# Sending for constants, attention weights and row vectors after the first tile's x has landed

## The chip, the cores and the metric
The kernel runs on one core of a Trainium2 chip. The metric is the device time of one execution in microseconds (us), smaller being better.

## The reference
For an input H of 16 batches x 512 tokens x 256 features (f32) the kernel computes

```
xn  = layernorm(x)                               # no gain, no bias
qkv = xn @ W_qkv.T + b_qkv ; q = elu(q)+1 ; k = elu(k)+1        # 16 heads of 16
att = (q @ (k.T @ v)) / clip(q . sum(k), 1e-6)                  # linear attention
a   = layernorm(att @ W_proj.T + b_proj) * gamma + beta + xn
h   = silu((xn @ w1.T) * s1) * ((xn @ w2.T) * s2)               # 256 -> 1024
h   = gelu((h @ h1.T) * t1) ; h = gelu((h @ h2.T) * t2)         # 1024 -> 1024, twice
out = x + a + (h @ w3.T) * s3                                   # 1024 -> 256
```

w1, w2, h1, h2 and w3 hold only -1, 0 and 1.

## The kernel before, in words
A tile is one batch of 512 tokens; 16 tiles go through a loop on every engine (`over_tiles`: a prologue for the first tile, then a body for each). Every engine has its program written out by hand, and the engines are tied by semaphores alone. The FFN weights (11.5 MB) stay in SBUF for the whole run. An activation that enters a matmul is split in two parts (high bits and remainder), so the attention projections are three matmuls per product (lines 391 to 393) and an FFN product is two (L386).

In the body the attention steps of the next tile stand between FFN groups, so TensorE always finds work. Only the first tile has a prologue in the open, and this is where the change lies:

- SyncE (SP) sends for the first tile's x (L296), then for the half of the row vectors that holds the k and v bias (L326, 256 KB, one row repeated on 128 partitions), the vectors of per-feature scales and the q bias (L327), the other row vectors (L328, 512 KB), and a first 176 KB piece of the raw weights (L306), which VectorE later checks for low bits.
- ScalarE (ACT) sends for the constants (L593: identity and head masks), the raw qkv weights (L594, 768 KB) and the raw projection weights (L595, 256 KB). It then waits for the qkv weights and casts them into their high part (L598). **Behind that it waits for the vectors (L599)**, and only then comes to `transposed_hi` (L627), the high part of the transposed xn.
- GpSimd (POOL) waits for x (L342), sends for the first 2 MB of the FFN weights (L346), computes the first tile's 1/sqrt(var) (L353) and sends for the other five pieces (L346 again).
- VectorE (DVE) waits for x, makes the layer norm (L708, L701, L703, L714), then the low part of the qkv weights (L850, after ScalarE's cast), then the low part of the transposed xn (L727).
- TensorE (PE) runs five warm-up matmuls (L377), waits for constants and xn, transposes xn (L401), waits for both parts of the qkv weights and of the transposed xn, and runs the projections of the first tile (L391 to L393); then the body begins.

The lines that a sentence can't replace are ScalarE's start:

```
593  act.dma_start(const[:], consts).then_inc(s_const, 16)
594  act.dma_start(wqkv_raw[:]..., w_attn[:, 0:DC * 3 * D]).then_inc(s_qkv_raw, 16)
595  act.dma_start(wproj_raw[:]..., w_attn[:, DC * 3 * D:]).then_inc(s_proj_raw, 16)
597  act.wait_ge(s_qkv_raw, 16)
598  nc.scalar.activation(wqkv[:, 0], wqkv_raw[:], ACT.Copy).then_inc(s_hi_w, 1)
599  act.wait_ge(s_vec, 16)
```

Of the kernel before, what the change touches and what calls it, by code (L numbers as in the profile page):

```python
# [98 lines left out]
def block_kernel(nc, H, w_ffn, w_attn, vecs, rows, consts, out):  # L99
# [70 lines left out]
    def sem(name):  # L170
        return nc.alloc_semaphore(name)
# [23 lines left out]
    x_loaded = Count(sem("x_loaded"), 1, unit=16)  # L195
# [77 lines left out]
    def over_tiles(eng, first, prologue, body):  # L273

        prologue(first)
        with eng.Fori(first, first + B - 1) as t:
            body(t, True)
        body(first + B - 1, False)

    def second_pass_if_needed(eng, run):  # L280
        eng.wait_ge(s_flag, 1)
        need = eng.value_load(flag[0:1, 0:1])
        with eng.If(need != 0):
            run()

    block = nc.Block()
    with block:


        @block.sync  # L290
        def _(sp):
            sp.sem_inc(acc_free.sem, 1)

            def load_x(t, first):
                sp.wait_ge(acc_made.sem, acc_made.at(t - 1, TC - 1))
                sp.dma_start(x[:], of_tile(x_dram, t - first)).then_inc(x_loaded.sem, 16)  # L296

            def of_tile(dram, tile):
                return dram[tile] if isinstance(tile, int) else dram[bass.ds(tile, 1)][0]

            def body_of(first):
                def load_piece(t, j):
                    sp.wait_ge(piece_checked.sem, piece_checked.at(t, j - 1))
                    col = (t * CHECKS + j) * CHECK_COLS
                    src = w_ffn[:, col:col + CHECK_COLS] if isinstance(col, int) else w_ffn[:, bass.ds(col, CHECK_COLS)]
                    sp.dma_start(raw[:], src.bitcast(U32)).then_inc(piece_loaded.sem, 16)  # L306

                def body(t, more):
                    if first == 0:
                        load_piece(t, 0)  # L310
                    if more:
                        load_x(t + 1, first)
                    if first == 0:
                        for j in range(1, CHECKS):
                            load_piece(t, j)
                    for half in range(2):
                        two = slice(2 * half, 2 * half + 2)
                        sp.wait_ge(out_made.sem, out_made.at(t, half))
                        sp.dma_start(of_tile(out_dram, t - first)[:, two], acc[:, two]).then_inc(out_stored.sem, 16)
                    sp.wait_ge(out_stored.sem, out_stored.at(t, 1))  # L320
                    sp.sem_inc(acc_free.sem, 1)
                return body

            def prologue(t):
                load_x(t, 0)
                sp.dma_start(rowv[:, R_BKV:], rows[:, R_BKV:].to_broadcast([P, 2 * D])).then_inc(s_bias_kv, 16)  # L326
                sp.dma_start(vec[:], vecs).then_inc(s_vec, 16)  # L327
                sp.dma_start(rowv[:, :R_BKV], rows[:, :R_BKV].to_broadcast([P, R_BKV])).then_inc(s_rows, 16)  # L328

            over_tiles(sp, 0, prologue, body_of(0))  # L330

            def second():
                sp.dma_start(w_full[:], w_ffn).then_inc(s_reload, 16)
                over_tiles(sp, B, lambda t: load_x(t, B), body_of(B))
            second_pass_if_needed(sp, second)
# [254 lines left out]

        @block.scalar
        def _(act):
            act.dma_start(const[:], consts).then_inc(s_const, 16)  # L593
            act.dma_start(wqkv_raw[:].rearrange("p k n -> p (k n)"), w_attn[:, 0:DC * 3 * D]).then_inc(s_qkv_raw, 16)  # L594
            act.dma_start(wproj_raw[:].rearrange("p k n -> p (k n)"), w_attn[:, DC * 3 * D:]).then_inc(s_proj_raw, 16)  # L595
# [402 lines left out]
```

## Time and profile before

| what | value |
|---|---|
| device time, median of 3 runs | 1606.58 us (1605.88 to 1607.11) |
| span of the profiled execution, first to last instruction | 1605.2 us |
| TensorE busy | 99% of the span |
| mean granted TensorE clock | 0.997 |
| x of the first tile, from issue to landing | 7.4 us |
| same transfer for the other tiles | 3.4 to 3.7 us |

The profiled execution has no device time of its own beside its span; the span is 1.4 us under the median of the timed runs. A span runs from the first instruction to the last. In the profile a DMA is issued by an engine's sequencer (SPq, ACTq, POOL) and is worked off by 16 DMA engines that all queues share: queue q1 is SP's, q10 is ACT's, q0 is POOL's. A "packet" of the DMA views is one piece of a transfer: here a stretch that is contiguous on one partition. x has four of 1 KB on each of 128 partitions; the other loads have one on each, so 128 packets, 8 on each of 16 engines.

### The profile page before, as it was taken

What the parts mean: (1) busy time and instruction counts of PE and PEld (TensorE: products, weight loads), DVE (VectorE), ACT (ScalarE), POOL (GpSimd) and SP (SyncE); (2) the same over time, 40 slices, a digit from 0 to 9 for tenths busy, and PEclk for the clock granted to TensorE, in tenths of its full rate; (3) what the DMA queues carried; (4) which work ended last, traced back from release to release, by engine and by line L of the source; (5) the groups of instructions that cost most, each with busy time, mean ns of one, the idle gap of its engine ahead of it and who ended that gap; (6) DMA issues with size and microseconds to landing.
All of it is one profiled execution on the core that took longest, in us unless ns stands there. A gap on an engine that the chain in (4) does not pass through costs nothing.

```text
span 1605.2 us, 22443 instructions
## 1 busy us (share of the span) xinstructions
PE 1591.0 (99%) x7884; PEld 1326.0 (83%) x7884; DVE 945.4 (59%) x1927; ACT 527.6 (33%) x817; POOL 38.1 (2%) x44
## 2 busy tenths in 40 slices
PE   8999999999999999999999999999999999999998
PEld 5888888888888888888888888888888888888886
DVE  5656657466564656647566474664746646566563
ACT  3324142241423424233242332423324143241421
POOL 1000000000000000000000000000000000000000
PEclk9999999999999999999999999999999999999999
DMA  9000000000000000000000000000000000000000
GB/s 355 23 12 11 27 18 22 11 11 27 18 22 18 4 27 18 22 22 0 27 18 27 18 9 18 18 27 18 18 9 18 27 18 22 11 11 27 18 10 20
DMA packets 28114, 42.07 MB, mean 26 GB/s; under 512 B 2112, under 2 KB 26816, under 8 KB 27328
## 3 DMA queue, kind: packets, MB, share of 16 engines
q1 hardware_dynamic: 26800, 29.12, 5.7%
q0 software_dynamic: 864, 11.53, 1.8%
q10 hardware_dynamic: 432, 1.18, 0.2%
q8 instruction: 10, 0.16, 0.0%
q14 instruction: 8, 0.07, 0.0%
HBM read 33.44 MB, written 8.39 MB: 26 GB/s over the span
## 4 chain that ended last, share of the span: by engine, by line
PE 99%; DMA 0%; DVE 0%; POOL 0%; issue 0%; DVEq 0%; POOLq 0%
PE ps L386 74%; PE ps L519 7%; PE ps L391 4%; PE ps L392 4%; PE ps L393 4%; PE ps L442 2%; PE ps L431 2%; PE ps L452 1%; PE ps L401 1%; DMA x<-in_H 0%; DVE wqkv_parts L850 0%; DVE xn L714 0%; DVE bn_stats L708 0%; POOL rstd L353 0%; DVE xn L837 0%
## 5 line engine op out<-in xcount | busy, mean ns | idle before, releaser
L386 PE MATMUL ps<-hidden_a,w_ffn 128*128 128x512 f32 x2048 | 488.1, 397 | 0.0
L386 PE MATMUL ps<-hidden_b,w_ffn 128*128 128x512 f32 x2048 | 484.4, 396 | 0.0
L386 PEld LDWEIGHTS ps<-hidden_b,w_ffn 128*128 128x128 f32 x2048 | 383.5, 188 | 91.6
L386 PEld LDWEIGHTS ps<-hidden_a,w_ffn 128*128 128x128 f32 x2048 | 381.4, 188 | 88.5
L622 ACT ACTIVATE value_ring<-ps,vectors 128x512 f32<-128x512 f32 x256 | 173.1, 689 | 693.7 <-PE ps L386 684.4
L386 PE MATMUL ps<-xnT,w_ffn 128*128 128x512 f32 x1024 | 249.4, 398 | 0.0
L386 PEld LDWEIGHTS ps<-xnT,w_ffn 128*128 128x128 f32 x1024 | 190.1, 188 | 43.6
L803 DVE CAST hidden_a<-value_ring 128x512 fp32r<-128x512 f32 x128 | 54.5, 426 | 216.0 <-ACT value_ring L622 216.0
L789 DVE SCALAR_TENSOR_TENSOR value_ring<-ps,vectors,gate_ring 128x512 f32<-128x512 f32 x128 | 94.2, 746 | 83.5 <-ACT gate_ring L604 83.5
L519 PEld LDWEIGHTS ps<-w_ffn,hidden_a 128*128 128x128 f32 x1024 | 123.9, 188 | 2.9
L519 PE MATMUL ps<-w_ffn,hidden_a 128*128 128x256 f32 x1024 | 124.6, 279 | 0.0
L803 DVE CAST hidden_b<-value_ring 128x512 fp32r<-128x512 f32 x128 | 54.5, 425 | 113.6 <-ACT value_ring L622 113.3
L604 ACT ACTIVATE gate_ring<-ps,vectors 128x512 f32<-128x512 f32 x128 | 86.7, 689 | 99.2 <-PE ps L386 99.0
L805 DVE TENSOR_TENSOR hidden_b<-value_ring,hidden_b 128x512 fp32r<-128x512 f32 x128 | 88.6, 692 | 4.4
L805 DVE TENSOR_TENSOR hidden_a<-value_ring,hidden_a 128x512 fp32r<-128x512 f32 x128 | 88.6, 692 | 4.4
L794 DVE TENSOR_TENSOR hidden_a<-value_ring,hidden_a 128x512 fp32r<-128x512 f32 x128 | 87.4, 683 | 2.2
L609 ACT ACTIVATE hidden_a<-value_ring 128x512 fp32r<-128x512 f32 x128 | 80.0, 625 | 9.7 <-DVE value_ring L789 9.7
L639 ACT ACTIVATE exp_tmp<-zkv 128x256 f32<-128x256 f32 x64 | 26.8, 418 | 150.1 <-DVE zkv L739 150.1
L845 DVE SCALAR_TENSOR_TENSOR low_bits<-raw_weights,low_bits 128x352 uint32<-128x352 uint32 x64 | 33.5, 523 | 68.7 <-DMA raw_weights<-in_w_ffn 68.7
L353 POOL TENSOR_TENSOR rstd<-var_plus_eps,power 128x4 f32<-128x4 f32 x32 | 34.3, 1072 | 1503.1 <-DVE var_plus_eps L703 1503.1
L739 DVE TENSOR_TENSOR zkv<-ps,row_vectors 128x512 f32<-128x512 f32 x64 | 44.3, 692 | 22.4 <-PE ps L393 22.4
L837 DVE TENSOR_TENSOR xn<-ps,row_vectors 128x512 f32<-128x512 f32 x32 | 22.1, 692 | 49.3 <-PE ps L519 49.3
(76 smaller groups left out, 1338.8 us busy)
## 6 DMA issues: line engine op xcount, KB each, us to landing
raw_weights<-in_w_ffn SPq DMA_DIRECT2D x64, 176.0 KB, 2.3
w_ffn<-in_w_ffn POOLq DMA_DIRECT2D x5, 2048.0 KB, 14.0
x<-in_H SPq DMA_DIRECT2D x16, 512.0 KB, 3.6
out_dram<-acc SPq DMA_DIRECT2D x32, 256.0 KB, 2.2
w_ffn<-in_w_ffn POOLq DMA_DIRECT2D x1, 1024.0 KB, 24.6
wqkv_raw<-in_w_attn ACTq DMA_DIRECT2D x1, 768.0 KB, 5.5
row_vectors<-in_rows SPq DMA_DIRECT2D x1, 512.0 KB, 7.8
wproj_raw<-in_w_attn ACTq DMA_DIRECT2D x1, 256.0 KB, 6.8
```

Of the source, the lines that this page charges most:

```text
L386: r = mm(bank, a, b, start=first and part == 0, stop=last and part == 1)
L391: mm(bank, wl, xh, start=first, stop=False)
L392: mm(bank, wh, xl, start=False, stop=False)
L393: return mm(bank, wh, xh, start=False, stop=last)
L519: r = mm(pair_bank(g, j)[:, 0:D], f(a) if full else a, wk, start=k == 0 and part == 0, stop=k == HC - 1 and part == 1)
L604: nc.scalar.activation(gate[:, o % 2, :], pair_bank(o, 0), ACT.Silu, scale=vec[:, V_GATE + o:V_GATE + o + 1]).then_inc(silu_made.sem, 1)
L609: nc.scalar.activation(ha[:, o, 0, :], val[:, o % 2, :], ACT.Copy).then_inc(gate_hi.sem, 1)
L622: nc.scalar.activation(val[:, n % 2, :], pair_bank(g, j), ACT.Gelu, scale=vec[:, col:col + 1]).then_inc(gelu_made.sem, 1)
L789: v.scalar_tensor_tensor(out=val[:, o % 2, :], in0=pair_bank(o, 1), scalar=vec[:, V_UP + o:V_UP + o + 1], in1=gate[:, o % 2, :], op0=ALU.m ...
L794: v.tensor_tensor(ha[:, o, 1, :], val[:, o % 2, :], ha[:, o, 0, :].bitcast(F32), ALU.subtract).then_inc(split.sem, 1)
L803: v.tensor_copy(dst[:, o, 0, :], val[:, n % 2, :]).then_inc(hid_hi.sem, 1)
L805: v.tensor_tensor(dst[:, o, 1, :], val[:, n % 2, :], dst[:, o, 0, :].bitcast(F32), ALU.subtract).then_inc(split.sem, 1)
```

## The change
SP waits for the first x to have landed before it issues its three other loads of the prologue, and ACT waits for the same before it issues its three. The order within each queue stays, and no load, size or arithmetic changes. POOL's wait for x stood there before.

```diff
             def prologue(t):
                 load_x(t, 0)
+                sp.wait_ge(x_loaded.sem, x_loaded.at(t, 0))
                 sp.dma_start(rowv[:, R_BKV:], rows[:, R_BKV:].to_broadcast([P, 2 * D])).then_inc(s_bias_kv, 16)
                 sp.dma_start(vec[:], vecs).then_inc(s_vec, 16)
                 sp.dma_start(rowv[:, :R_BKV], rows[:, :R_BKV].to_broadcast([P, R_BKV])).then_inc(s_rows, 16)
...
         def _(act):
+            act.wait_ge(x_loaded.sem, x_loaded.at(0, 0))
             act.dma_start(const[:], consts).then_inc(s_const, 16)
             act.dma_start(wqkv_raw[:].rearrange("p k n -> p (k n)"), w_attn[:, 0:DC * 3 * D]).then_inc(s_qkv_raw, 16)
             act.dma_start(wproj_raw[:].rearrange("p k n -> p (k n)"), w_attn[:, DC * 3 * D:]).then_inc(s_proj_raw, 16)
```

On ScalarE, at the very start of its program, before the change (with what each instruction waits for):

```order
L593 DMA constants<-in_consts 128x264
L594 DMA wqkv_raw<-in_w_attn 128x1536
L595 DMA wproj_raw<-in_w_attn 128x512
L598 ACT_TABLE_LOAD
L598 ACTIVATE wqkv_parts<-wqkv_raw 128x1536 [waits qkv_weights_loaded]
L627 ACTIVATE xnT<-ps 128x512 [waits attention_step_ready,vectors_loaded]
```

The same place now (line numbers are two higher behind the two new lines):

```order
L595 DMA constants<-in_consts 128x264 [waits x_loaded]
L596 DMA wqkv_raw<-in_w_attn 128x1536
L597 DMA wproj_raw<-in_w_attn 128x512
L600 ACT_TABLE_LOAD
L600 ACTIVATE wqkv_parts<-wqkv_raw 128x1536 [waits qkv_weights_loaded]
L629 ACTIVATE xnT<-ps 128x512 [waits attention_step_ready,vectors_loaded]
```

The first DMA of the three has gained the wait, and all that stands behind it on ScalarE is held with it.

On SyncE, the start of its program now; before, the second row had no wait and nothing else was different:

```order
L296 DMA x<-in_H 128x4x256 [waits acc_made]
L327 DMA row_vectors<-in_rows 128x512 [waits x_loaded]
L328 DMA vectors<-in_vecs 128x34
L329 DMA row_vectors<-in_rows 128x1024
```

The loads of the row vectors and vectors, and the raw weights' first piece behind them, have moved behind x's landing. GpSimd's start, with the same wait in both kernels (here as it is now):

```order
L347 DMA w_ffn<-in_w_ffn 128x4096 [waits x_loaded]
L354 ISA
L354 TENSOR_TENSOR rstd<-var_plus_eps,power 128x4 [waits ln1_var_plus_eps,power_made]
L347 DMA w_ffn<-in_w_ffn 128x4096 x4
L347 DMA w_ffn<-in_w_ffn 128x2048
```

Nothing has moved within it, but three queues now wait for one event.

## Rows read from the trace of the kernel before

**Rows 1.** The page: span, and shares of the chain that ended last.
```profile
span 1605.2 us, 22443 instructions
...
PE 99%; DMA 0%; DVE 0%; POOL 0%; issue 0%; DVEq 0%; POOLq 0%
```

**Rows 2.** The chain, 0 to 45 us: start us, length us, what.
```profile
1.20 7.40 DMA x<-in_H
...
12.00 1.38 DVE xn L714 x4
13.38 1.67 DVE wqkv_parts L850
15.05 0.66 DVE xnT L727
...
15.84 0.76 PE ps L391
...
21.30 0.43 PE ps L391
...
21.97 0.23 PE ps L393
...
27.16 3.73 PE ps L386 x16
```

**Rows 3.** Timeline, 0 to 45 us: start, length, engine, line, operation.
```profile
0.75 0.39 ACTq L593 DMA_DIRECT2D constants<-in_consts  x1
...
1.18 0.45 ACTq L594 DMA_DIRECT2D wqkv_raw<-in_w_attn  x1
...
1.69 0.51 SPq L326 DMA_DIRECT2D row_vectors<-in_rows  x1
...
2.25 0.43 SPq L327 DMA_DIRECT2D vectors<-in_vecs  x1
...
6.67 1.48 ACT L598 ACTIVATE wqkv_parts<-wqkv_raw 128x1536 fp32r<-128x1536 f32 x1 [3.17 <-DMA wqkv_raw<-in_w_attn]
...
8.90 0.71 POOL L346 DMA_DIRECT2D w_ffn<-in_w_ffn  x1 [8.01 <-DMA x<-in_H]
...
11.94 2.83 POOL L346 DMA_DIRECT2D w_ffn<-in_w_ffn  x5
...
14.37 1.08 ACT L627 ACTIVATE xnT<-ps 128x512 fp32r<-128x512 f32 x2 [6.22 <-PE ps L401]
```

**Rows 4.** DMA issues, 0 to 45 us: transfer, queue, KB each, us to landing.
```profile
wqkv_raw<-in_w_attn ACTq DMA_DIRECT2D x1, 768.0 KB, 5.5
...
vectors<-in_vecs SPq DMA_DIRECT2D x1, 17.0 KB, 7.1
```

**Rows 5.** x of the other tiles: DMA time from issue to landing.
```profile
DMA to landing us min/median/max: 3.4/3.6/3.7
```

**Rows 6.** DMA queues, 3.5 to 5 us: packets, MB, share of 16 engines.
```profile
q10 hardware_dynamic: 75, 0.46, 84.7%
q1 hardware_dynamic: 64, 0.07, 12.7%
```

**Rows 7.** DMA queues, 8.6 to 10 us.
```profile
q1 hardware_dynamic: 223, 0.49, 89.5%
```

**Rows 8.** DMA queues, 10 to 12 us.
```profile
q0 software_dynamic: 31, 0.51, 92.7%
q1 hardware_dynamic: 29, 0.03, 4.3%
```

**Rows 9.** DMA queues, 13 to 35 us: all packets, then queue q0.
```profile
DMA packets 640, 9.44 MB, mean 429 GB/s; under 512 B 64, under 2 KB 64, under 8 KB 64
...
q0 software_dynamic: 640, 9.44, 103.0%
```

**Rows 10.** Stretches: us, busy of PE, PEld, DVE, ACT, POOL, PEclk, DMA share, GB/s.
```profile
8.00:14.80 6.80, 2.86 (x13) 1.35 (x11) 4.75 (x14) 0.58 (x2) 4.54 (x7) 1.00 1.01 367
14.80:21.65 6.85, 5.81 (x14) 4.58 (x15) 2.18 (x4) 2.28 (x5) 0.00 (x0) 0.50 1.02 426
```

## The prediction
> **What bounds the kernel now.** I read the page first: the chain that ended last lies on TensorE for 99% of a span of 1605.2 us [rows 1]. Nothing that runs beside TensorE in the loop can matter, and the change touches nothing in the loop. What it can move is the head, the time before TensorE runs without a gap. So I read the chain of waits over the first 45 us [rows 2]. It is x's transfer (issued at 1.20, 7.40 us, landed at 8.60), the layer norm (xn done at 13.38), the low part of the qkv weights (L850, until 15.05), the low part of the transposed xn, and TensorE's first projection at 15.84. From there on TensorE has work to the end. So one number prices the change: by how much the first projection's start moves away from 15.84 us. Each us there is a us of the time.
>
> The head's transfer of x is slow. The same 512 KB take 3.4 to 3.7 us in the later tiles [rows 5], against 7.4. The DMA queues between 3.5 and 5 us show why: ACT's queue q10 moved 75 packets and 0.46 MB, SP's q1 64 packets and 0.07 MB [rows 6]. The queues start about one packet each in turn, whatever the size. A qkv row has 6 KB and a piece of x has 1 KB, so x gets an eighth of the bytes while the qkv weights move. This is what the change sets out to remove, and the same counting tells what it puts in its place.
>
> **What it removes.** Alone, x lands 3.6 us after its issue [rows 5], at 4.8 instead of 8.60: 3.8 us earlier. The layer norm follows it (4.8 us from landing to the last xn in [rows 2]), so xn is done at 9.6 instead of 13.38. If all else were in time, the first projection would start at 12.0.
>
> **What it adds.** Three engines are released by that landing. ACT issues the constants at about 4.9 and, at the 0.43 us spacing of [rows 3], the qkv weights at 5.3. SP issues the bias rows at 4.9 and the vectors at 5.45 (0.56 us after them, as in [rows 3]). POOL, which waited for x before too, issues 2 MB of FFN weights 0.3 us after landing (8.90 against 8.60 in [rows 2, 3]), at 5.1; from 8.6 to 10 us q1 is alone [rows 7], its own first data comes after 10 us [rows 8], 1.1 to 1.6 us behind the issue, so now at about 6.5. Its other five pieces were issued 3.3 us after x (11.94 [rows 3]), so now at 8.1, before the first is worked off. Queue q0 therefore has work without a break from 6.5 on. Before, it first had data when the small loads were all but done: 29 packets of q1 were left [rows 8]. **Now all small loads share the DMA engines with it.**
>
> The price of sharing comes from packets. From 13 to 35 us q0 moved 640 packets, 64 of them tiny: 576 packets of 16 KB in 22 us on 16 engines, at a share of 103% [rows 9]. That is 22 x 16 x 1.03 / 576 = 0.63 us for one packet on its engine. In [rows 6] a 6 KB packet takes 0.847 x 1.5 x 16 / 75 = 0.27 us, and one of 1 KB 0.127 x 24 / 64 = 0.05. I estimate 0.09 for 2 KB from this. Each load of 128 rows has 8 packets on each engine.
>
> Qkv weights: data from about 6.6 (1.3 us after the issue, in the middle of what POOL's and SP's first data show). A round of one packet from each queue is 0.63 + 0.27 + 0.09 = 0.99 us, eight rounds 7.9 us, so they end near 14.6; with the constants ahead and some tenths until the semaphore, **landing is at 15.2**. The cast on ScalarE (1.48 [rows 3]), L850 (1.7), L727 (0.66) and 0.15 until TensorE starts [rows 2] add 4.1: the projection could start at 19.3. Before, the cast was over at 8.2 and L850 ran beside the transposes.
>
> Vectors: they stand in SP's queue behind the bias rows, so sixteen of its packets per engine have to go, and ScalarE waits for them (L599) ahead of the transposed xn. Eight rounds of 0.99 bring the bias home at about 14.7; eight more with the projection weights (0.63 + 0.09 + 0.02 = 0.74) take 5.9. **The vectors land at about 21.0.** Then come half of L627's 1.08 [rows 3], L727's 0.66 and 0.15: the first projection starts at 22.4. That is the latest of the waits, so **22.4 - 15.84 = 6.6 us are lost**.
>
> Hidden edits. The constants are ahead in ACT's queue; even at eight full rounds of 0.63 + 0.05 + 0.09 they land near 12.5, before the vectors, so they cost nothing while these are late. ScalarE's table load falls into the wait for the weights. The other row vectors take eight more rounds, to about 28. VectorE wants them after the last of the first tile's projections, which end 11.3 us after they begin (27.16 against 15.84 [rows 2]), so at 33.7; covered. The FFN weights gain about 5 us of start and lose about 6 us of engine time to small loads; the first 2 MB are there by 15, wanted at 33.7 too. The raw piece is wanted in the FFN's second stage.
>
> **The clock.** At 14.80 to 21.65 the granted clock was 0.50, with 5.81 us of TensorE work in it, after a stretch in which it was busy for 2.86 of 6.80 us [rows 10]. Matmuls were 0.43 us apart until 21.30 and 0.23 after [rows 2]: about 13 matmuls at the lower level, 2.6 us lost. TensorE now idles longer before 22.4, so I expect such a stretch again and take 0. Bounds: -2.6 (full clock at once) and +3.1 (a second stretch, 6.85 us at 0.23 instead of 0.43).
>
> The sum: 1605.2 + 6.6 = 1611.8 for the span; against the median of 1606.58, which lies 1.4 over that span, 1613.2. I say 1613.0.
>
> On the turn-taking the Trainium skill ("DMA: Bandwidth & Descriptors", section "Queues, rings and completion order") says otherwise: an engine goes round the queues but drains a whole packet of about 9 to 17 descriptors from one before it switches. The 75 to 64 of [rows 6] speak for single pieces. What the rule would make of the sum is the second rival.
>
> **The rivals.** (1) *Only the qkv weights are late.* The vectors' packets (17 KB in 128, so 136 bytes, [rows 4]) might pass several in a turn. Against it is the nearly even count of [rows 6]. The start is then 19.3, +3.5, and up to +5 if a longer half-clock stretch follows: 1610.1 to 1611.6. (2) *Turns of a whole piece.* If an engine works off all 8 packets of an FFN piece (8 x 0.63 = 5.0 us) before it turns to others, q0 holds it from 6.5 to 11.5, the qkv weights (2.2) and bias rows (0.7) follow until 14.4, another 5.0, and the vectors land near 19.8: start 21.2, +5.4, 1612.0. This is what that section of the Trainium skill would do here. (3) *Equal bytes.* If queues share by bytes, qkv weights and constants (0.92 MB) land when three times that has moved, 6.5 us at 429 GB/s [rows 9], at 13.2: start 17.3, +1.5, of which an earlier end of the half clock may give back 0.6: 1607.5 to 1608.1. [rows 6] speak against it too: 0.46 MB against 0.07. (4) *The small loads slip in ahead of POOL's*, the case for a gain. [rows 8] show that POOL's data starts slowly: 31 packets in 2 us, where 16 engines at 0.63 could do 50. Then the qkv weights need no more than their 5.5 us of before [rows 4]: landing at 10.8, start at 14.9, 0.9 us gained, 1605.7. At best they land in 3.8 us, the start is 13.3 (2.5 gained), and TensorE, which idles less, keeps its full clock (2.6 more): 1601.5. The change decides for a gain where the qkv weights land before 11.7 (15.84 - 4.1) and the vectors before 14.4.
>
> **How the numbers follow.** A difference of 0.2%, 3.2 us, is about what a measurement of this kernel can tell from no change. Chances: my forecast 0.52, rival 1 0.12, rival 2 0.09, rival 3 0.13, rival 4 0.14 of which 0.04 gains over 3.2 us. Slower needs a start after 19.0: forecast, rivals 1 and 2, less a little, 0.72; faster 0.04; the rest 0.24. The forecast's own range is 1610.5 to 1616.5 by the clock's bounds. For 8 in 10 the range reaches down to rival 3 and the weaker part of rival 4: 1606.0 to 1616.5.
>
> **What would show it.** x lands 3.4 to 4.2 us after its issue. The issue of the qkv weights to landing is 9 to 10 us instead of 5.5, that of the vectors about 15 instead of 7.1 [rows 4]. ScalarE sits idle between L598 and L627 until the vectors land, and the chain of waits goes over the vectors or the qkv weights, not over x and the layer norm. Between 7 and 14 us q0 and q10 start packets in equal numbers. The first projection is near 22.4, and the loop's stretches keep their length. I am wrong if qkv weights land before 12, or the vectors before 16, or if the half-clock stretch vanishes or doubles.

## The result, and the profile after

The changed kernel takes 1608.92 us in the median (1607.22 to 1609.98, 20 runs) against 1606.13 of before (1604.79 to 1607.68, 20 runs): a ratio of 1.0017, 95% interval 1.001 to 1.0024, so 2.8 us slower. I had forecast 1613.0, 6.4 us above the median known then. The direction is right, the size is less than half of it, and at 0.17% the loss stays under the 0.2% that I had set for "slower". It lies in my wide range (1606.0 to 1616.5), which reached down there for rivals 3 and 4, and below the range of the forecast itself (1610.5 to 1616.5). Of all executions reported here one is slow, one of experiment 5's twelve at 5604.08 us, for a reason that no trace shows, and the ratio of experiment 5 leaves it out.

The page of the changed kernel: the span, and the chain by engine.

```profile
span 1605.4 us, 22443 instructions
...
PE 99%; DMA 1%; DVE 0%; ACT 0%; issue 0%; ACTq 0%; DVEq 0%
```

TensorE still holds the chain [rows 1]. The chain of waits of the changed kernel, 0 to 45 us, to be set against [rows 2]; columns are start, length, what.

```profile
1.20 3.43 DMA x<-in_H
4.65 0.39 ACTq L595
...
5.07 9.19 DMA wqkv_raw<-in_w_attn
14.29 1.49 ACT wqkv_parts L600
15.80 1.76 DVE wqkv_parts L852
17.56 0.61 DVE xnT L729
...
18.31 0.76 PE ps L392
...
28.84 3.73 PE ps L387 x16
```

x lands at 4.63 instead of 8.60, as the change intends. But the chain no longer goes from x to the layer norm. It goes over the qkv weights, sent for at 5.07 instead of 1.18 and 9.19 us on their way. ScalarE's cast stands behind them in the open, where before it was over at 8.15, during x's transfer. VectorE's L852 follows it; that step (L850 before) was on the chain before too, behind the layer norm. The first projection starts at 18.31 instead of 15.84, 2.47 us later, and the first FFN group at 28.84 instead of 27.16, 1.68 later. DMA issues of the changed kernel, 0 to 45 us (transfer, queue, KB, us to landing; compare [rows 4, 5]):

```profile
wqkv_raw<-in_w_attn ACTq DMA_DIRECT2D x1, 768.0 KB, 9.2
x<-in_H SPq DMA_DIRECT2D x1, 512.0 KB, 3.4
...
row_vectors<-in_rows SPq DMA_DIRECT2D x1, 256.0 KB, 5.0
...
constants<-in_consts ACTq DMA_DIRECT2D x1, 132.0 KB, 5.2
vectors<-in_vecs SPq DMA_DIRECT2D x1, 17.0 KB, 5.7
```

The vectors took 5.7 us, not about 15 as forecast. The DMA queues of the changed kernel at 4 to 8, at 8 to 9.3 and at 9.3 to 13.2 us (packets, MB, share of 16 engines) say why:

```profile
q1 hardware_dynamic: 160, 0.25, 31.5%
q10 hardware_dynamic: 68, 0.07, 6.1%
...
q10 hardware_dynamic: 103, 0.29, 56.9%
q1 hardware_dynamic: 125, 0.05, 22.6%
...
q0 software_dynamic: 59, 0.97, 59.2%
q10 hardware_dynamic: 115, 0.57, 35.7%
```

POOL issued its 2 MB at 4.93, but its queue q0 shows nothing until 9.3 us. I had put its first packet at 6.5. By 9.3 the bias rows and most of the vectors had gone. Only the rest of the qkv weights met the 16 KB packets, and these came in slowly: from 9.5 to 10.5 us q0 started 11 packets and q10 41; only from 10.5 to 13 us are the counts near each other, 39 and 50.

### The profile page after: what moved, and what is told of

Read it like the earlier page. It is cut to its first block, busy times and chain, and to the rows that moved or that the text cites. A ratio compares the mean times of both kernels' runs of the same rounds, so it can differ in the third digit from the quotient of the medians.

```text
span 1605.4 us, 22443 instructions
## 1 busy us (share of the span) xinstructions
PE 1590.4 (99%) x7884; PEld 1325.3 (83%) x7884; DVE 945.2 (59%) x1927; ACT 527.5 (33%) x817; POOL 38.1 (2%) x44
## 3 DMA queue, kind: packets, MB, share of 16 engines
q10 hardware_dynamic: 432, 1.18, 0.2%
## 4 chain that ended last, share of the span: by engine, by line
PE 99%; DMA 1%; DVE 0%; ACT 0%; issue 0%; ACTq 0%; DVEq 0%
PE ps L387 74%; PE ps L520 7%; PE ps L392 4%; PE ps L393 4%; PE ps L394 4%; PE ps L443 2%; PE ps L432 2%; PE ps L453 1%; PE ps L402 1%; DMA wqkv_raw<-in_w_attn 1%; DMA x<-in_H 0%; DVE wqkv_parts L852 0%; ACT wqkv_parts L600 0%; DVE xn L839 0%; DVE acc L842 0%
## 5 line engine op out<-in xcount | busy, mean ns | idle before, releaser
L741 DVE TENSOR_TENSOR zkv<-ps,row_vectors 128x512 f32<-128x512 f32 x64 | 44.3, 692 | 22.4 <-PE ps L394 22.4
```

## The experiments

All medians are against the kernel before in the same comparison. "First projection" and "first FFN group" are from each kernel's chain of waits.

| kernel | first projection | first FFN group | time against before | ratio, 95% interval |
|---|---|---|---|---|
| before | 15.84 | 27.16 | | |
| the change | 18.31 | 28.84 | +2.8 us | 1.0017 (1.001 to 1.0024) |
| 1: only ScalarE waits | 23.65 | 34.57 | +6.5 | 1.0041 (1.0028 to 1.0055) |
| 2: only SyncE waits | 16.38 | 26.56 | -0.5 | 0.9997 (0.9988 to 1.0006) |
| 3: FFN pieces after the qkv weights | 16.34 | 27.66 | -0.3 | 1.0 (0.9991 to 1.0009) |
| 4: SyncE's loads after the qkv weights | 28.51 | 39.24 | +12.6 | 1.0087 (1.0071 to 1.0102) |
| 5: qkv weights behind x in one queue | 15.57 | 26.91 | -0.4 | 0.9995 (0.9986 to 1.0004) |
| 6: first FFN piece at once | 19.70 | 30.52 | +3.9, one run | |
| 7: first FFN piece in 4 KB packets | 16.82 | 27.21 | +0.8 | 1.0005 (0.9997 to 1.0014) |
| 8: all but the constants behind x in one queue | 12.29 | 21.20 | -5.9 | 0.9963 (0.9949 to 0.9976) |
| 9: as 4, vectors right behind x | 17.24 | 27.58 | +0.6 | 1.0003 (0.9993 to 1.0012) |
| 10: FFN piece alone after x | 29.50 | 40.87 | +14.9, one run | |

One number carries the table: the time follows the first FFN group's start to about 1.2 us in every row. The loop behind it doesn't move. From the start of the first FFN group to the start of the last addition it takes 1599.33 - 27.16 = 1572.17 us before, 1601.01 - 28.84 = 1572.17 after, 1593.38 - 21.20 = 1572.18 in experiment 8.

**Experiments 1 and 2: each wait alone.** The first drops SyncE's wait, the second ScalarE's:

```diff
             def prologue(t):
                 load_x(t, 0)
-                sp.wait_ge(x_loaded.sem, x_loaded.at(t, 0))
```

```diff
-            act.wait_ge(x_loaded.sem, x_loaded.at(0, 0))
```

> Only ScalarE's loads wait for x; SyncE sends for bias rows, vectors and other row vectors right behind x, as before the change. Theory A (the qkv weights are late because their descriptors are made behind those of SyncE's loads, 3.1 us from issue to first data, and because the FFN pieces' 16 KB packets then share the engines from 9.4 us): x lands near 4.7 us, the qkv weights' first data comes about 1.5 us after their issue at 5.1, they land near 9.5 to 10.5, the first projection starts near 13.5 to 14.5, and the kernel is 1 to 2.5 us faster than before the change. Theory B (sharing with the FFN pieces alone sets the landing): the weights land at 12.5 or later and the first projection starts at 16.5 or later, slower than before by 1 us or more.

> Only SyncE's three loads wait for x; ScalarE's go out at once, as before the change. x shares the engines with the qkv weights and lands at 7.5 to 8.6 us, the weights land at 6.7. Theory A (the loss of the change lies in ScalarE's wait): first projection at 15.0 to 15.9, time within 1 us of before. Theory B (the vectors, behind the bias rows, meet the FFN pieces round by round): the vectors land after 14.5 and the first projection starts after 16.

ScalarE's wait alone is worse than both together. Theory B of experiment 1 holds; nothing that I wrote for theory A came true but x's landing (at 4.87). In this kernel SyncE's loads go out right behind x and keep q1 busy alone, and the small loads of ScalarE come last. DMA queues of experiment 1 at 5.3 to 7.1, then at 12 to 18.4 us:

```profile
q1 hardware_dynamic: 211, 0.48, 100.3%
...
q0 software_dynamic: 153, 2.24, 83.9%
q10 hardware_dynamic: 150, 0.41, 17.7%
```

The first row shows SyncE's loads with the engines to themselves for 2 us after ScalarE's constants were issued (4.88). Then ScalarE's packets meet the FFN pieces one for one, 150 to 153, and the qkv weights need 14.3 us. With SyncE's wait alone (2), x again shares with the qkv weights and lands at 8.68, and nothing is lost or won: the vectors landed 4.4 us after their issue. That is theory A by the time, though the first projection is 0.5 us later than it allowed. So the loss is ScalarE's wait, and SyncE's wait takes part of it away. The constants, ahead of the qkv weights in their queue, landed at 12.8 us in experiment 1 and at 9.9 in the changed kernel, and q0's first packet came at 8.7 against 9.4 us. From 9.5 to 10.5 us the queues of experiment 1, then of the changed kernel, read:

```profile
q0 software_dynamic: 17, 0.28, 70.0%
q10 hardware_dynamic: 21, 0.11, 29.5%
...
q10 hardware_dynamic: 41, 0.24, 58.6%
q0 software_dynamic: 11, 0.18, 43.4%
```

So the qkv weights get through in the changed kernel before q0 takes its full turns. Why q0 comes in later and more slowly there is part of the open question further down.

**Experiment 3: the FFN pieces held back.**

```diff
-            load_weights(0)
...
                 ln1(t)
-                for i in range(1, len(w_pieces)):
+                pool.wait_ge(s_qkv_raw, 16)
+                for i in range(len(w_pieces)):
```

> The changed kernel, with GpSimd sending for all FFN pieces only when the qkv weights have landed, so that nothing of 16 KB a packet shares the engines with them. Theory A (sharing costs): the weights land at 10.8 to 12 us instead of 14.3, the first projection starts at 14.9 to 16.1 instead of 18.3, and the kernel is 1.5 to 3.5 us faster than the changed one. Theory B (they are late only by their issue and by descriptors made in one line): landing stays within 1 us of 14.3 and nothing is won.

The qkv weights landed at 5.14 + 7.16 = 12.3 and the first projection started at 16.34: sharing with the FFN pieces cost the change about 2 us of landing. Theory A holds in kind; landing and start lie up to 0.3 us past its bounds. Even without the pieces the wait gains nothing over before, since 7.16 us of transfer start only after x. The landing of the qkv weights, at 6.7 us before and at 14.3 now, thus moved in three parts: 3.9 us for the later issue, 1.7 us because they took 7.2 us instead of 5.5 even without an FFN piece, beside the small loads that were let go with them, and 2.0 us for the FFN pieces.

**Experiments 4, 9 and 10: the vectors, and turns between queues.** These test the step of my forecast that did not happen. Each is an edit of the changed kernel, the first two on SyncE (4, then 9), the third on both engines (10).

```diff
-                sp.wait_ge(x_loaded.sem, x_loaded.at(t, 0))
+                sp.wait_ge(s_qkv_raw, 16)
```

```diff
-                sp.wait_ge(x_loaded.sem, x_loaded.at(t, 0))
+                sp.dma_start(vec[:], vecs).then_inc(s_vec, 16)
+                sp.wait_ge(s_qkv_raw, 16)
                 sp.dma_start(rowv[:, R_BKV:], ...)
-                sp.dma_start(vec[:], vecs).then_inc(s_vec, 16)
```

```diff
-                sp.wait_ge(x_loaded.sem, x_loaded.at(t, 0))
+                sp.wait_ge(ln1_var.sem, ln1_var.at(t, 0))
...
-            act.wait_ge(x_loaded.sem, x_loaded.at(0, 0))
+            act.wait_ge(ln1_var.sem, ln1_var.at(0, 0))
```

> The changed kernel, but SyncE's three loads wait for the qkv weights instead of x, so that the vectors (sixteenth packet of each engine in their queue) meet the FFN pieces in full. The qkv weights, alone with the constants, should land at 9 to 10.5 us. Theory A, the one on record (one packet from each queue in turn, whatever its size, 0.7 us a round with an FFN packet in it): the vectors land 11 to 13 us after the bias rows' issue, near 22 us, and the first projection starts near 23.5, 5 us later than in the changed kernel. Theory B (small packets pass several at a time): the vectors land 5 to 6 us after issue, near 16, and the first projection starts near 17.

> The kernel in which SyncE's loads wait for the qkv weights, but with the vectors sent for at once behind x, so that only the bias rows and the other row vectors meet the FFN pieces. Theory A (the 12.6 us that it lost were the vectors' wait alone): ScalarE goes on as soon as the weights are cast, the first projection starts at 15.3 to 16.3 us, the time is within 1.5 us of before. Theory B (the bias rows are late as well): the first projection is early but VectorE waits for the bias rows at L739 and the time is 3 us or more over before.

> The changed kernel, but SyncE's and ScalarE's loads wait for the layer norm's variance (near 6.8 us) instead of x's landing, so that GpSimd's first DMA, issued near 4.95, has the engines to itself. In the changed kernel its first packet came 4.5 us behind the issue, on record I had 1.1 to 1.6. Theory A (it is held back by the small loads that are issued at the same moment): first packet of its queue before 6.8 us; then ScalarE's constants meet 16 KB packets, their first packet comes over 3 us behind the issue, and everything on record follows: qkv weights near 16 to 20 us, vectors after them, first projection after 21 us. Theory B (GpSimd's first DMA needs 3 us or more whenever it is issued early): first packet after 7.9 us.

In experiment 4 the vectors, 17 KB, took 15.2 us, the time that I had forecast for the change. Its chain of waits:

```profile
11.83 15.19 DMA vectors<-in_vecs
27.04 0.61 ACT xnT L629
27.67 0.70 DVE xnT L729
...
28.51 0.77 PE ps L392
```

And its DMA queues at 14.8 to 21.4 (bias rows), then at 21.5 to 26.4 us (vectors, 136 bytes a packet):

```profile
q0 software_dynamic: 164, 2.33, 88.3%
q1 hardware_dynamic: 153, 0.26, 11.3%
...
q0 software_dynamic: 132, 1.93, 94.6%
q1 hardware_dynamic: 140, 0.05, 6.1%
```

A packet of 136 bytes waits its turn behind one of 16 KB just as one of 2 KB does. Theory A holds in kind, but the vectors landed at 27.0 us, 5 later than it said: the qkv weights had landed 1 us late, the queue's first packet came over 3.2 us behind the issue at 11.44, and sixteen turns took some 12 us, 0.77 each. Experiment 9 frees the vectors alone from this and takes 12 us back. It missed its start by 1 us: the qkv weights landed at 13.2, in experiment 4 at 11.4. q0 had three packets before 8.3 us here and none there; whether that accounts for 1.8 us is open. Experiment 10 moves the small loads 2 us away from POOL's issue (4.85). Its queues at 6.2 to 6.8, 7.2 to 10.5, and 17.5 to 24 us:

```profile
q0 software_dynamic: 15, 0.25, 174.4%
...
q0 software_dynamic: 80, 1.31, 100.1%
...
q0 software_dynamic: 137, 1.98, 72.9%
q10 hardware_dynamic: 139, 0.77, 28.6%
q1 hardware_dynamic: 138, 0.02, 3.5%
```

Between 4.5 and 6.2 us no packet moved at all, so q0's first one came 1.4 to 1.9 us behind the issue, what I had forecast for the change. The small loads, issued from 6.76 on, had no packet by 10.5: 3.7 us and more, against about 1 us for the constants before. Then the three queues take turns evenly, 137, 139 and 138 (some of them of 4 bytes; q0's 1.98 MB are 121 pieces of 16 KB). The qkv weights took 18.3 us, more than the 9 to 13 of theory A, and landed at 25.5.

Two more things can be read there. First, the constants had their own eight turns: from 10.5 to 17.4 us q0, q1 and q10 started 143, 135 and 133 packets, while q10 moved just 0.14 MB; the qkv weights, behind them in the queue, had theirs from 17.5 on. Second, even counts over 6 us would also come out if each queue had its eight packets worked off in one go. A short stretch tells the two apart. Experiment 10 at 19.1 to 19.4 us:

```profile
q10 hardware_dynamic: 13, 0.08, 63.3%
q0 software_dynamic: 7, 0.02, 14.1%
q1 hardware_dynamic: 13, 0.00, 5.8%
```

One qkv packet takes 0.633 x 0.3 x 16 / 13 = 0.23 us on its engine, so eight in one go would take 1.9 us, and eight of the vectors 0.2. Yet in 0.3 us q10 and q1 start 13 each (q0 one piece of 16 KB), and from 19.42 to 20 us again 13 each, now with 14 pieces of q0. Turns of one packet give that; turns of eight would not keep the queues in step.

**Experiment 6: the first FFN piece without its wait for x.** The line `pool.wait_ge(x_loaded.sem, ...)` is removed.

> The changed kernel, but GpSimd sends for the first 2 MB of the FFN weights at once, without its wait for x. It asks when that queue's first data comes. Theory A (a fixed delay of up to 4.5 us behind the issue): first 16 KB packet at 2.3 to 5.5 us, x is caught in rounds of 0.67 us and lands at 8 us or later. Theory B (GpSimd's descriptors aren't ready before some 8 us into the run, whenever it issues): first packet at 8 us or later and x lands at 4.6 us as in the changed kernel.

The 2 MB were issued at 1.30. q0 showed no packet up to 3.9 us (x's 457 alone) and 16 in the next 0.3, as x's ran out; x landed at 4.62, undisturbed. It is between my two theories: delayed about 2.7 us, neither past 8 us nor a bar to x. Behind it, q0 was alone from 5 to 8.2 us and the small loads came late again.

**Experiment 7: the same FFN piece in smaller packets.**

```diff
-            load_weights(0)
+            for lo in range(0, W_HID1, HID):
+                pool.dma_start(w[:, lo:lo + HID], w_ffn[:, lo:lo + HID]).then_inc(s_w[0], 16)
...
-                        pe.wait_ge(s_w[0], 16)
+                        pe.wait_ge(s_w[0], 64)
```

> The changed kernel with the first 2 MB of the FFN weights sent for in four DMAs of 4 KB rows instead of one of 16 KB rows, so that a round of one packet from each queue costs 0.16 us of FFN data instead of 0.63. Theory A (packets in turn): the qkv weights land 1 to 2 us earlier than 14.3, the first projection starts at 16.3 to 17.3, and the kernel is 0.7 to 2 us faster than the changed one. Theory B (bytes in turn, or no effect of packet size): landing within 0.5 us of 14.3 and no gain.

The qkv weights landed at 5.13 + 7.65 = 12.8 and the projection started at 16.82: theory A. Its median, 1606.87, is 2.4 us under the change's in the same comparison (1609.27), a little more than the 0.7 to 2 that I had written, for the same bytes. The size of the neighbour's packet is what the others pay for.

**Experiments 5 and 8: order in one queue in place of a wait.** Both start from the kernel before. In 5 ScalarE keeps the projection weights, in 8 it sends for the constants alone (the two wproj_raw lines below are of 8).

```diff
                 load_x(t, 0)
+                sp.dma_start(wqkv_raw[:]..., w_attn[:, 0:DC * 3 * D]).then_inc(s_qkv_raw, 16)
+                sp.dma_start(vec[:], vecs).then_inc(s_vec, 16)
                 sp.dma_start(rowv[:, R_BKV:], ...)
-                sp.dma_start(vec[:], vecs).then_inc(s_vec, 16)
                 sp.dma_start(rowv[:, :R_BKV], ...)
+                sp.dma_start(wproj_raw[:]..., w_attn[:, DC * 3 * D:]).then_inc(s_proj_raw, 16)
...
-            act.dma_start(wqkv_raw[:]..., w_attn[:, 0:DC * 3 * D]).then_inc(s_qkv_raw, 16)
-            act.dma_start(wproj_raw[:]..., w_attn[:, DC * 3 * D:]).then_inc(s_proj_raw, 16)
```

> No engine waits for x before it issues; instead the qkv weights move from ScalarE's queue to SyncE's, right behind x, so that the order within one queue gives x the engines first and the weights next. Theory A (what counts is the order in which packets get the engines, and a wait for landing only wastes time and hands it to the FFN pieces): x lands at 4.6 to 5.6 us, the weights at 7 to 8.5, before any FFN piece moves, L850 follows the layer norm at once, the first projection starts at 12 to 13.5 us instead of 15.84, and the kernel is 1.5 to 4.5 us faster than before. Theory B (x is slowed by whatever moves): x lands later than 6.5 us and the first projection starts after 14.5, a gain under 1.3 us.

> Like the one-queue kernel, but the projection weights too stand in SyncE's queue, after the row vectors; ScalarE sends for the constants alone, at once, and no engine waits for x before it issues. In the one-queue kernel x took 7.1 us with only the constants and the 256 KB of projection weights on the other queue. Theory A (any sizeable transfer on the other queue slows x, one behind it in its own queue doesn't): x lands at 4.6 to 5.5 us, the qkv weights at 6.8 to 8.5, the first projection starts at 12 to 13 us, the kernel is 2 to 4.5 us faster than before. Theory B (x is slowed by what stands behind it in its own queue): x lands after 6.5 us and the gain is under 1.5 us.

Experiment 5 failed, as its theory B says: x took 7.1 us with 256 KB on the other queue. Experiment 8 is theory A and beats the kernel before by 5.9 us and so the changed one by some 8.7. Its chain of waits:

```profile
1.20 3.85 DMA x<-in_H
...
8.45 1.38 DVE xn L714 x4
9.83 1.67 DVE wqkv_parts L850
11.50 0.66 DVE xnT L727
...
12.29 0.47 PE ps L393
...
21.20 3.74 PE ps L388 x16
```

Here x lands at 5.05 and the weights, right behind it with no wait between, 5.4 us after their issue at 1.69, before the layer norm is done. It is the chain of [rows 2], 3.6 us earlier. The projections take 21.20 - 12.29 = 8.9 us instead of 11.3, since TensorE does not fall to its lower level there; these 2.4 us are why the gain is above the 2 to 4.5 that I had written. Stretches 8 to 14.8 and 14.8 to 21.65 us of experiment 8, to be set against [rows 10] (PEclk, the third number from the end, is 1.00 in both):

```profile
8.00:14.80 6.80, 4.94 (x23) 3.23 (x22) 4.29 (x7) 2.52 (x5) 3.22 (x6) 1.00 1.06 423
14.80:21.65 6.85, 6.85 (x30) 5.12 (x29) 4.46 (x9) 3.98 (x9) 0.00 (x0) 1.00 1.03 429
```

**The change profiled again.**

> The changed kernel once more, for a second profile. In the first, the first FFN group starts 1.68 us later than before the change, the medians differ by 2.8 us. Theory A (the profiled execution was a favourable one in its last microseconds, and the clock's stretch falls otherwise in others): first FFN group again 1.5 to 3 us later than 27.16, and the time from the last addition to the end of the span varies by 1 to 1.5 us between profiles. Theory B (something in the loop is slower): the distance from the first FFN group to the last output group changes from 1563.9 us.

> The kernel before the change once more, for a second profile: the first projection at 15.5 to 16.2 us, the first FFN group within 0.7 us of 27.16, and another length of the stretch between the last addition and the end of the span (5.2 us in the first profile, 3.6 to 5.1 in those since).

The second profile of the change (1609.27 us, ratio 1.002, 1.0011 to 1.0028) has the first projection at 18.74 and the first FFN group at 29.76. The second of before has 16.02 and 27.27. The loss at the FFN group is thus 1.7 us in one pair and 2.5 in the other, against 2.8 in the medians. The distance to the last output group is unchanged: 1592.77 - 28.84 = 1563.93 in the first profile of the change, as 1591.09 - 27.16 before. Between the last addition's end and the span's end lie 5.2 us in the first profile of before and 3.7 in the three others; so the spans 1605.2 and 1605.4 of the two first profiles look alike although the head does not. The change's first profile is also of its fastest execution, 1607.22. Where the 1.5 us at the end come from is not shown.

## Why the prediction was wrong, point by point

- **x alone: right.** 3.4 us from issue to landing (forecast 3.6).
- **The time of the whole is that of the first projection's start: right in kind.** The loop's length is the same to 0.01 us.
- **The qkv weights: near in number, partly by luck.** Landing at 14.26 (forecast 15.2), projection possible from 18.31 (19.3). Experiments 1 and 2 show that ScalarE's wait brings the loss, 3 and 7 that turns with 16 KB packets are part of it. But I had eight full turns with them from 6.6 us on. By 8 us q10 had moved 68 packets of the constants and nothing of the weights, q0 came at 9.4, and the FFN pieces cost 2.0 us in all. My sum was also at odds with its own rule. The constants are ahead in the same queue, and I let them take eight full turns, to 12.5, in one paragraph and "some tenths" in another. In experiment 10, where q0 was there in time, they did take their eight turns and the qkv weights landed at 25.5. Counted in full, my rule would have put the landing in the change near 20 (an estimate: eight rounds of 0.92 to 0.99 us behind 12.5); that the small loads ran ahead of q0 hid this.
- **The failed step: "its own first data comes after 10 us, 1.1 to 1.6 us behind the issue, so now at about 6.5", and with it "the vectors land at about 21.0".** POOL's first packet came 4.5 us behind its issue. When it came, most of the vectors' packets had gone, and they landed at 10.7. So they were never the last wait, and 22.4 became 18.3. The rule for the turns was right: experiment 4 gave the vectors 15.2 us. Experiment 10, in which POOL's data did start by 6.8 us, has the first projection at 29.50, later than my 22.4 even with its 2 us of later issue taken off. There the small loads' own first packets came over 3.7 us behind the issue, where I had 1.3, and the constants' turns add to it. What failed is that I carried over a start-up time from a place where the small loads were nearly done to one where they were all being sent for.
- **The chances.** No rival came true whole. The outcome is rival 1's, only the qkv weights late (0.12), but not for its reason, packets that pass several in a turn, and not at its price (1610.1 to 1611.6). The reason is rival 4's, small loads that slip in ahead of POOL's slow start (0.14), without the gain that I hung on it. Against rival 1 I held a packet count that was right but didn't apply, since I hadn't doubted the time at which the counting begins; and I saw POOL's slow start but took from it only the 1.1 to 1.6 us.
- **The clock.** I took 0 with bounds of -2.6 and +3.1. The projections took 28.84 - 18.31 = 10.5 us instead of 11.3 in the first profiles, 11.0 against 11.25 in the second: 0.2 to 0.8 us back. The lower stretch came again, from about 15.1 to 21.9 us in the first profile and longer, from 13.2 to 23.3, in the second (granted clock 0.50 in both), but more of it had passed before TensorE had work. Experiment 8 shows the bound itself: no lower stretch, 2.4 us.
- **Turns of a whole piece (rival 2), equal bytes (rival 3): refuted.** Against rival 3 stand the bytes of experiments 4 and 10 (1.98, 0.77 and 0.02 MB in one stretch), against rival 2 the counts in step within 0.3 us of experiment 10. The Trainium skill ("DMA: Bandwidth & Descriptors", section "Queues, rings and completion order") has an engine drain a whole packet of about 9 to 17 descriptors from one queue before it switches. The trace does not agree: one packet each, 13 to 13, and here the measurement decides.
- **The case for a gain (rival 4)** needed the weights before 11.7. They landed at 12.3 even without any FFN piece beside them (experiment 3), so with these two waits there was nothing to be had. With SyncE's loads held back instead they landed at 11.4, but then the vectors were late (experiment 4). Both held back at once, with the vectors sent first, was not run.

Not settled: why POOL's first packet is so late. From issue to first packet it took 1.4 us before, 1.4 in experiments 3 and 10, 1.5 in 5, 1.9 in 2, 2.7 in 6 (beside x alone), 3.1 in 9, 3.4 in 4, 3.6 in 1, 4.2 in 7, 4.5 in the change and 4.8 in 8. In experiment 8 all small loads had been issued before POOL's piece at 5.35, so it doesn't take an issue at the same moment. Small packets still outstanding go with most of the long delays, but are not enough either: in experiment 5 q1 started 277 packets between POOL's issue at 8.63 and its first packet at 10.15 and 192 more until 13 us, and the delay was 1.5 us. VectorE's work does not account for it: in all these kernels but 3 and 6 POOL issues 0.3 us behind x's landing, as the layer norm begins, whether the delay is 1.4 or 4.8 us. No run isolates the cause.

## What to carry to other kernels

Before a transfer is held back by a wait, list what its queue and the others will hold when it is let go: here the wait freed x in 3.4 us and put 768 KB, needed within 5 us, beside 16 KB packets of weights that nobody needed for 20 us. To give one transfer the engines, put the next ones behind it in the same queue and keep large loads off the other queues (experiment 8). There the order cost x 0.4 us (3.85 against 3.43); the wait for landing sent the qkv weights off 3.9 us later than before, and their start-up came on top. And a start-up time read at one place of a trace holds for the traffic of that place: check what the engines were doing there.

## What the runs showed of the hardware

- Queues that all have packets ready take turns by single packets, whatever their size: 137, 139 and 138 packets from three queues that moved 1.98, 0.77 and 0.02 MB (experiment 10), and 13 and 13 within 0.3 us. While a queue is starting up the counts are not even: 11 to 41 in the changed kernel, and the case below.
- A new transfer from SyncE or ScalarE shows its first packet over 3.7 us after its issue when 16 KB packets hold the engines (experiment 10), against about 1 us when they are idle. Small packets delay it too: 2.3 us for the constants of experiment 1, beside SyncE's loads alone, and 2.3 us for x before, beside the constants and the qkv weights.
- 256 KB on a second queue made x take 7.1 us instead of 3.9; queues of experiment 5 at 3 to 4.5 us:

```profile
q10 hardware_dynamic: 65, 0.12, 65.1%
q1 hardware_dynamic: 14, 0.01, 20.5%
```

x hardly got a turn there, 14 packets to 65. The engines were busy for 86% of that time and yet moved just 93 GB/s: a packet of q10, most of them 2 KB, took 0.651 x 1.5 x 16 / 65 = 0.24 us, where I had estimated 0.09. By even turns x would have lost 8 x 0.09 = 0.7 us. Why these packets are slow, and why x starts so late beside them, is open.
